# A language-model tower on one core: one rotary rotation for a head's query and key, projected three heads ahead, and softmax reciprocals kept in PSUM

## What is computed

```python
def _rope(x, cos, sin):
    xr, xi = jnp.split(x, 2, -1)
    return jnp.concatenate([xr * c - xi * s, xr * s + xi * c], -1)

def _attn(q, k, v, mask=None):
    s = jnp.einsum('bhqd,bhkd->bhqk', q, k) / np.float32(np.sqrt(HD))
    ...
    return jnp.einsum('bhqk,bhkd->bhqd', jax.nn.softmax(s, -1), v)

qr = _rope((cq @ Wq_rope)..., cos, sin)         # 16 heads, rotary part 64 wide
q = jnp.concatenate([qn, qr], -1)
# three attentions with their own keys; the window's and the selected keys are rotated too;
# their outputs are summed with the weights gate (softmax over three), then projected with Wproj
```

## Time and profile before

| | |
|---|---|
| median of 3 executions | 1830.76 us (1827.94 to 1831.23) |
| the profiled execution | 1832.47 us |
| its span, first to last instruction | 1830.7 us |
| busy share of the span | PE 78%, DVE 78%, ACT 67%, POOL 78% |
| mean granted TensorE clock | 0.959 of full speed |

### The profile page before, as it was taken

How to read it: one execution, slowest core, us unless ns; L and a number is a source line. 1 busy time by engine, 2 the same in 40 slices (tenths; PEclk the granted TensorE clock), 3 DMA queues, 4 the chain that set the end, 5 groups by cost and what they waited for, 6 DMA issues and landing times.

```text
span 1830.7 us, 62295 instructions
## 1 busy us (share of the span) xinstructions
PE 1423.3 (78%) x19368; PEld 1150.3 (63%) x19368; DVE 1436.5 (78%) x4989; ACT 1225.4 (67%) x3280; POOL 1437.0 (78%) x2126
## 2 busy tenths in 40 slices
PE   1041488888888888888888888888888888888778
PEld 0021377767777777777777776777767776766643
DVE  5747678887888788878887888888887888778845
ACT  0041277777777787778877777777767877777644
POOL 6775489877887899789987889788878997899610
PEclk9985699999999999999999999999999999999989
DMA  5110132223222322232222222222222222323200
GB/s 93 22 26 2 35 71 57 52 45 64 52 52 45 71 52 56 46 64 52 53 51 64 53 52 57 56 53 52 55 60 53 52 56 42 60 62 69 54 4 20
DMA packets 327634, 93.11 MB, mean 51 GB/s; under 512 B 321104, under 2 KB 323024, under 8 KB 327520
## 3 DMA queue, kind: packets, MB, share of 16 engines
q1 hardware_dynamic: 324448, 88.48, 24.9%
q0 software_dynamic: 3072, 3.15, 0.9%
HBM read 6.51 MB, written 1.05 MB: 4 GB/s over the span
## 4 chain that ended last, share of the span: by engine, by line
POOL 60%; issue 17%; DVE 10%; PE 8%; POOLq 2%; DMA 2%; ACT 1%; DVEq 0%; ACTq 0%; SPq 0%
POOL big L425 9%; POOL big L424 9%; POOL kparts L460 7%; POOL big L394 5%; POOL vh L480 4%; POOL qparts L446 4%; POOL kparts L457 4%; POOL kk L428 3%; POOL kk L429 3%; POOL qs L428 3%; POOL qs L429 3%; DVE S L1008 3%; POOL osum L473 2%; POOL qparts L449 1%; PE S L1356 1%
## 5 line engine op out<-in xcount | busy, mean ns | idle before, releaser
L635 ACT ACTIVATE big<-S,negm 128x128 f32<-128x128 f32 (+3 forms) x1536 | 577.4, 450 | 196.8 <-DVE negm L1008 195.7
L647 ACT ACTIVATE big<-PT 128x384 f16<-128x384 f32 (+3 forms) x1024 | 426.6, 455 | 150.7 <-PE PT L1381 112.2
L1018 DVE SCALAR_TENSOR_TENSOR big<-PT,big 128x384 f16<-128x384 f32 (+3 forms) x1024 | 472.1, 500 | 39.1 <-ACT big L647 26.3
L1008 DVE CUSTOM_DVE_ANT_0 S<-S,mask_c,unscale 128x128 f32<-128x128 f32 (+3 forms) x512 | 285.1, 557 | 182.8 <-PE S L1356 176.6
L1356 PE MATMUL S<-k1T,qh 128*128 128x128 f16 (+3 forms) x1536 | 296.8, 302 | 113.9 <-DMA qh<-qparts 98.0
L1356 PE MATMUL S<-kh,qh 128*128 128x128 f16 (+1 forms) x3072 | 323.3, 242 | 0.0
L1403 PEld LDWEIGHTS O<-vh,big 128*128 128x128 f16 x8064 | 272.7, 96 | 41.9 <-issue 14.3
L1403 PE MATMUL O<-vh,big 128*128 128x33 f16 x8064 | 283.3, 178 | 14.7 <-DVE big L1030 8.0
L1356 PEld LDWEIGHTS S<-kh,qh 128*128 128x128 f16 x3072 | 229.9, 99 | 56.0
L1388 PE MATMUL PT<-cst,big 128*128 128x128 f32 x1408 | 248.6, 281 | 16.8 <-DVE big L1018 15.1
L1381 PE MATMUL PT<-cst,big 128*128 128x128 f32 x1280 | 232.6, 281 | 19.1 <-DVE big L1018 17.4
(11 more groups left out here) (298 smaller groups left out, 2399.7 us busy)
## 6 DMA issues: line engine op xcount, KB each, us to landing
lat_b<-lat_all SPq DMA_DIRECT2D x8, 448.0 KB, 3.1
qh<-qparts SPq DMA_TRANSPOSE x128, 3.0
kh<-kparts SPq DMA_TRANSPOSE x128, 3.4
xnT_all<-xnT_b SPq DMA_DIRECT2D x14, 128.0 KB, 2.5
xn_b<-xn_all SPq DMA_DIRECT2D x8, 128.0 KB, 2.9
xnT_b<-xnT_all SPq DMA_DIRECT2D x8, 128.0 KB, 2.4
out_dram<-h_all SPq DMA_DIRECT2D x8, 128.0 KB, 2.0
xn_all<-xn_b SPq DMA_DIRECT2D x7, 128.0 KB, 2.0
```

The costliest lines, as they stand in the source:

```text
L635: last = nc.scalar.activation(pr[par][:, lo:lo + n], S[par][:, lo:lo + n], ACT.Exp, bias=negm[par][:, k:k + 1], scale=-1.0)
L647: last = nc.scalar.activation(pT[par][:, 0, lo:lo + n], PT[:, lo:lo + n], ACT.Copy, scale=PSCALE)
L1008: last = v.tensor_tensor_reduce(out=z, in0=z, in1=m, scale=unscale[:] if k == 0 else kfix[:], scalar=3.0e38, op0=ALU.add, op1=ALU.min, acc ...
L1018: v.scalar_tensor_tensor(pT[par][:, 1, lo:lo + n], PT[:, lo:lo + n], PSCALE, pT[par][:, 0, lo:lo + n], ALU.mult, ALU.subtract).then_inc(s[ ...
```

## The change

Three things, in one kernel.

1. **One rotation for a head's query and key.** `qs[par]` and `kk[par]` become two parts of one tile `qk[par]` of 9 tiles. The cosine table gets 9 tiles instead of 5, the sine table is copied into a 9-tile one by two copies on POOL before the first rotation. `prepare` runs one `rope` over all 9 tiles in the place of two, and then splits the key, then the query. The first two heads of each batch still rotate query and key apart.
2. **Three heads ahead.** K and Q of head `h + 3` stand in units 2 and 3 of the turn of head `h`, in the place of head `h + 2` in units 0 and 1. Their copies on ACT and the copy in `high_values` move along. The third head's projections, `qp2` and `kp2`, join the list `LEAD`; `project_rows` moves from units 2 and 3 to units 0 and 1, `half_residual` to unit 1, and PE's wait for it to the start of unit 2. POOL's order within a head is now `low_values`, `branch_sum`, (`normalise`), `prepare`.
3. **Reciprocals in PSUM.** `rinv` is no SBUF tensor any more but 12 unused columns of the PSUM tile `O`.

```diff
-        qs = [sb(f"qs{i}", [P, NT, QW]) for i in range(2)]
-        kk = [sb(f"kk{i}", [P, 5, P]) for i in range(2)]
+        qk = [sb(f"qk{i}", [P, NT + 5, P]) for i in range(2)]
+        qs, kk = [q[:, 0:NT] for q in qk], [q[:, NT:NT + 5] for q in qk]
...
-        rinv = sb("rinv", [P, NT, 3])
...
+        rinv = O[:, NT * 3 * (VD + 1):NT * 3 * (VD + 2)]
...
-        LEAD = ["cq", "qp0", "sel", "k1", "kp0", "qp1", "kp1"]
-        NX = (NH - 2) * 2 + len(LEAD)
+        LEAD = ["cq", "qp0", "sel", "k1", "kp0", "qp1", "kp1", "qp2", "kp2"]
+        NX = (NH - 3) * 2 + len(LEAD)
...
-            def prepare(b, h, hh, par, rows=None):
-
-                x = xbase(b) + h * 2
-                key(par, b, hh, x + x_index(0, "kp"))
-                query(par, b, hh, x + x_index(0, "qp"))
+            def prepare(par, b, hh, x):
+
+                n = rope_count(b, hh, None)
+                g.wait_ge(s["x_evac"], x + 2)
+                rope(qk[par], rt9, cos9, sin9, n)
+                split_key(par, b, hh, n)
+                split_query(par, b, hh, n)
+
+            def cycle(b, h, par, rows=None, add=True):
+
+                low_values(par, b, h + 1)
+                if add:
+                    branch_sum(par, b, h - 1)
                 if rows is not None:
                     normalise(rows, xn_b[:])
-                low_values(1 - par, b, hh - 1)
+                prepare(par, b, h + 3, xbase(b) + h * 2 + x_index(0, "qp"))
...
-                v.reciprocal(rinv[:].rearrange("p t k -> p (t k)").unsqueeze(2), o3[:, :, VD:VD + 1]).then_inc(s["coef_chain"], 1)
+                v.reciprocal(rinv.unsqueeze(2), o3[:, :, VD:VD + 1]).then_inc(s["coef_chain"], 1)
...
-                    if last < 1 and t == 0:
-                        k_proj(h + 2, xb + x_index(0, "kp"))
-                    if last < 1 and t == 1:
-                        q_proj(h + 2, xb + x_index(0, "qp"))
-                    if back is not None and t >= 2:
-                        project_rows(back, p * 2 + t - 2, xb + 2)
+                    if back is not None and t < 2:
+                        project_rows(back, p * 2 + t, xb)
+                    if back is not None and t == 2:
+                        pe.wait_ge(s["h_done"], back * 2 + p + 1)
+                    if xb is not None and t == 2:
+                        k_proj(h + 3, xb + x_index(0, "kp"))
+                    if xb is not None and t == 3:
+                        q_proj(h + 3, xb + x_index(0, "qp"))
```

More of the change, by code:

```diff
@@ L419, in _ @@
                                 f.unsqueeze(2).to_broadcast([P, TILES, hi - lo]), ALU.mult).then_inc(s["lat_done"], 1)
[L421 to L429, removed]
+            g.tensor_copy(sin9[:, 0:NT], sin5[:, 0:NT]).then_inc(s["sin_ready"], 1)
@@ L663, in turn @@
                     u = p * NT + t
-                    if t == 0 and last < 1:
-                        evac_k(p, xb + x_index(0, "kp"), H + 1)
-                    if t == 1 and last < 1:
-                        evac_q(p, xb + x_index(0, "qp"), H + 1)
-                    if t == 2 and last < 2:
+                    if t == 1 and last < 2:
                         high_values(1 - p, b, h + 1)
+                    if t == 2 and xb is not None:
+                        evac_k(1 - p, xb + x_index(0, "kp"), H + 2)
+                    if t == 3 and xb is not None:
+                        evac_q(1 - p, xb + x_index(0, "qp"), H + 2)
                     if nxt is not None:
@@ L724, in behind @@
                 probs(0, 0, b, U)
+                if first:
+                    lead(LEAD.index("qp2"), nxt, b * NH)
+                lead(LEAD.index("kp2"), nxt, b * NH)
                 if not first:
@@ L729, in behind @@
                 probs(2, 2, b, U + 2)
-            for i in range(len(LEAD)):
+            for i in range(LEAD.index("qp2")):
                 lead(i, 0)
@@ L737, in heads @@
             def heads(b, rows=False):
-                with act.Fori(0, NH // 2 - 1) as hp:
+                with act.Fori(0, NH // 2 - 2) as hp:
                     for p in range(2):
                         turn(b, hp * 2 + p, xbase(b) + hp * 4 + p * 2, p, 0, rows=hp if rows and p == 1 else None)
+                turn(b, NH - 4, xbase(b) + (NH - 4) * 2, 0, 0)
+                turn(b, NH - 3, None, 1, 0, rows=NH // 2 - 2 if rows else None)
             def last_heads(b, nxt):
@@ L1123, in turn @@
                         maxima(u + 3, (t + 3) % NT, U + t + 3)
-                    if back is not None and t == 3:
+                    if back is not None and t == 1:
                         half_residual(back, p)
@@ L1448, in turn @@
                     values(u, t, p, U + t, H)
-                if back is not None:
-                    pe.wait_ge(s["h_done"], back * 2 + p + 1)
             def value(b, j):
@@ L1493, in behind @@
                 scores(0, 0, 0, H * NT)
+                if first:
+                    lead("qp2", b, nxt)
+                lead("kp2", b, nxt)
                 if not first:
@@ L1520, in heads @@
                              rows=hp if rows and p == 1 else None)
+                turn(NH - 4, b * NH + NH - 4, xbase(b) + (NH - 4) * 2, 0, 0)
+                turn(NH - 3, b * NH + NH - 3, None, 1, 0, rows=NH // 2 - 2 if rows else None)
             def hidden(b, chunks=(0, 1, 2, 3), between=None):
@@ L1541, in _ @@
             last.then_inc(s["rank_psum"], 1)
-            for kind in LEAD[2:]:
+            for kind in LEAD[2:LEAD.index("qp2")]:
                 lead(kind, 0, 0)
```

69 lines of the change are left out of this document (42 added, 27 removed).

## The result

The changed kernel takes **1761.9 us** (median; the kernel before has 1830.3 in the same series): ratio 0.9635, 95% interval 0.9619 to 0.9651. That is 68 us less; forecast were 76 less, 1755, with a range of 1733 to 1793. The profiled execution has 1769.7 us, with a span of 1767.9. One of the five executions took 1805.5 us, and like it the profiled ones of the experiments `e3`, `e6` and `e8` lie 33 to 44 us above the median of their kernel; in these three the granted clock is down behind the heads, so only what lies ahead of that stretch is read from them.

What follows compares the result with a forecast made beforehand. POOL was taken to bound the kernel at 11.00 us a head, then the PE-DVE-ACT round at 10.35. Savings of 56, 10 and 10 made 76 us, from 1832.5 to 1756.5, as a median 1755; range 1733 to 1793.

Steps and rivals of the forecast that it cites:

- The bound moves from POOL to the round of PE, DVE and ACT: Main case: heads fall from POOL's 11.00 us to the round's 10.35, with POOL at 10.1; chance 0.50.
- The rotation: On POOL: products save 0.42 us, sums 0.26, a gap 0.20; together 0.88 a head, leaving POOL's head at 10.1.
- The round: PE, ACT and DVE links from the end of M3 once round, K and Q included: sum 10.37, taken as 10.35 us.
- The old order was the looser one: The same walk in the old order skips K and Q: 9.2 us a head with a free C, hidden by POOL.
- POOL as the bound: Rival: POOL still bounds every head at 10.1 us because the round's hand-overs overlap; 1737 us, chance 0.17.
- The reciprocals: With a PSUM input C on DVE stops waiting for POOL and takes 0.22 us, 0.47 less; worth nothing in the old order.
- The rival in which C keeps its wait: C on DVE still waits for POOL, so each head has 10.8 us; 1799 us, chance 0.24 shared with the 9-tile rival.
- A batch: Heads and the late turn save 8.0 us a batch, 56 in seven; the batch's first turns 1.5 net, 10 in seven.
- The last batch: POOL gives back 1.75 us per pair of heads, where `normalise` also runs; six pairs make 10 us.
- 9 tiles without a saving: Rival: POOL's instruction over 9 tiles saves nothing, POOL's head 10.8 us; 1799 us, chance 0.24 shared with C's wait.
- Q waiting for K's copy: Slower rival: on PE, Q waits for ACT's copy of K from tile `X`; at 1.0 us of waiting 1858 us, chance 0.05.
- No change: Rival: the losses from Q's waiting just eat the gain; 1831 us, chance 0.04.

Runs made afterwards that it cites:

- e3: The kernel before with only the one rotation over 9 tiles, still two heads ahead, reciprocals in SBUF: 2000.4 us, ratio 1.0930.
- e6: The changed kernel with key and query rotated apart again, still three heads ahead, reciprocals in PSUM: 1804.9 us, ratio 0.9857.
- e8: The changed kernel with three more, unused reciprocals on DVE between C and the product: 1770.4 us, ratio 0.9669.
- e9: The changed kernel with one more POOL copy of 48 columns in every head (0.23 us): 1763.6 us, ratio 0.9645.
- e7: The changed kernel with K between T1 and V0 of unit 0, Q between S0' and T2 of unit 1, `project_rows` in units 2 and 3: 1730.6 us.
- e4: The changed kernel with K and Q back at the starts of units 0 and 1, still three heads ahead: 1735.2 us, ratio 0.9491.
- e10: e7 with POOL's instructions reordered, `branch_sum` split around the key and query splits, casts ahead of differences: 1721.6 us, ratio 0.9409.
- e12: e10 with ACT's copy of the query moved behind H2 of unit 1: 1713.1 us, ratio 0.9366.
- e2: The kernel before with only the reciprocals moved to PSUM: 1830.8 us, ratio 1.0001.
- e1: The changed kernel with the reciprocals back in an SBUF tensor, all else as changed: 1878.9 us, ratio 1.0261.
- e11: The changed kernel with two unused row maxima on DVE between C and the product, 0.66 us of delay: 1918.8 us, ratio 1.0483.
- e7s: e7 with the reciprocals back in an SBUF tensor: 1797.7 us, ratio 0.9822.

## Why the prediction was right, and where it was off

**The bound moves from POOL to the round of PE, DVE and ACT: right, in the middle of the batches.** The wait for the query's DMA went, POOL waits for ACT's copy, and the filler of `e9` is free there. In the last batch POOL stays the bound. With the undone rotation (`e6`) POOL bounds again.

**The rotation: right, a little small.** The products take 1.40 and 1.41 (forecast 1.38), the sums 0.79 (forecast 0.85), the whole 4.65 (4.71). POOL's head without foreign waits is 10.03 (`e7`), against 10.1, and 10.95 with two rotations: 0.92 gained where 0.88 was forecast.

**The round: right, link by link.** From the rows above: M3 1.35; from L1 to K, with T2 and V1 between, 1.76 (forecast 0.63 + 1.04); K 0.43; S1', T3 and V2 2.12; Q 0.66; S2' to M2' 1.30; M2' and L0' 1.75; R, C and the product 1.04. Sum 10.41, the forecast 10.37. The largest miss is 0.09, in the hand-over from L1 to T2: I had counted from L1's first half, but V1 comes behind T2's second part, which waits for the second half. The next round is 10.55, and over eleven heads the mean is 10.46 against 10.35. That makes 0.11 x 11 x 7 = 8 us of the 13 by which the profiled execution's gain fell short of the forecast 76.

**"The old order was the looser one": right in sign, too small in size.** `e4` and `e7` show it, and they land where the prediction had priced POOL as the bound (1737; measured 1735 and 1731). But the walk of 9.2 was too short. With POOL no longer bounding, the order with K and Q in the gaps takes 9.97 on average (`e10`), and 9.74 at its best here (`e12`).

**The reciprocals: the mechanism right, the size wrong.** C falls to 0.17 (0.22 forecast), and in the old order it is worth nothing (`e2`), as written. In the new order the prediction put it at 0.47 us a head, 44 us in all (1799 against 1755); undone it costs 117. Two things had been left out: with 1.41 us on POOL the wait would have grown to 0.7, and the clock falls behind PE's longer waits. The rival in which C keeps its wait was priced at 1799 and would have been 1879. Both errors lie outside of the forecast case, so they didn't touch the time.

**A batch: 8.1 gained, 9.5 forecast.** Eleven heads that are 0.11 longer than forecast make 1.2 of the 1.4 that are missing. PE's waits for the residual, 0.95 and 1.28 in the earlier trace rows, aren't gone: they stand in front of K, and measure 0.46 and 0.18. In the first turn S0' still waits 0.56 for the key's transfer.

```profile
413.32 0.34 PE L1381 MATMUL S<-k1T,qh 128*128 128x128 f16 x3 [0.56 <-DMA kh<-kparts]
...
415.49 0.50 PE L1337 MATMUL X<-wkw,xh 128*128 128x96 f16 x8 [0.46 <-DVE h_all L1132]
...
426.28 0.50 PE L1337 MATMUL X<-wkw,xh 128*128 128x96 f16 x8 [0.18 <-DVE h_all L1132]
```

**The last batch: right where it was argued.** A pair of heads gains 1.90 (1.75 forecast), six pairs 11, and it is POOL's gain, as argued. From the last of the `attended` rows to POOL's last key split the profiled execution gains 9.4; behind that it loses 2.1, which leaves the 7.3. Its granted clock from 1640 to 1700 us is 0.79; in the execution of `e9`, whose work there is the same but for the filler, it is 0.89, and the span is 4.8 shorter (first the changed kernel, then `e9`):

```profile
1640.00:1700.00 60.00, 46.58 (x507) 37.00 (x503) 39.20 (x140) 32.75 (x83) 24.63 (x43) 0.79 0.13 28
```

```profile
1640.00:1700.00 60.00, 42.86 (x508) 33.44 (x503) 41.96 (x151) 32.41 (x83) 25.58 (x46) 0.89 0.14 28
```

That goes some way to explain why this execution lies 7.8 above the median; what decides the clock in that stretch stays open.

**The rivals.** POOL as the bound: out in the middle of the batches, by `e9`. C with its wait, or 9 tiles without a saving: out, by the rows. Q waiting for K's copy: no wait stands ahead of Q. No change: out.

## What to carry to other kernels

Walk the next bound link by link before the first is removed: here it lay 0.5 us behind, and the new place of K and Q, chosen with the rotation, lay on it; the same change with K and Q in PE's idle stretches is 31 us faster. An edit's worth belongs to an order: the same twelve numbers in PSUM were worth 0, 67 and 117 us in three of them. Before an instruction on an in-order queue is made to wait for something later, look at what stands behind it: with `low_values` behind a waiting rotation (`e3`) PE waited 2.44 us for it in the head shown, more than the 0.88 that the rotation saves.

## What the runs showed of the hardware

- **The clock multiplies a wait.** PE waits of 0.4 and 0.6 to 0.8 us in a head left the granted clock at 1.00 in the middle of the batches (the changed kernel), 1.06 to 1.17 and 0.65 to 0.84 brought it to 0.50 for 2 to 3 us in about every second head (`e1`, `e11`). So 0.66 us more on the round (`e11`) cost 1.07 a head on average over eleven heads, and C's 0.7 (`e1`) cost 1.3. Waits of nearly the same length bring the clock down in one head and not in the next; nothing that I found in the rows tells the two apart, and it stays open.
- **C's wait ends with POOL's instruction**: between 430 and 1300 us all 168 rows of C over 0.3 us (the kernel before, `e1`, `e7s`) end 0.02 to 0.04 us behind a POOL instruction, whether that lasts 1.16 or 1.41; with one input in PSUM C took 170 to 171 ns on average in every run. The Trainium skill ("SBUF — State Buffer", Who interferes with whom) says that a VectorE instruction with two SBUF inputs contends with a GpSimd one that reads SBUF, and that the ports they share are an exclusive lock; the runs agree. Its larger latency for a PSUM source ("VectorE: DVE Perf Modes", The TRN2 errata) isn't seen in this instruction: 171 ns with PSUM, 170 at best in the earlier trace rows without.
- **Small DVE instructions overlap.** Three reciprocals of 12 columns, 0.20 us each by their rows, delayed the next instruction by 0.11 in all: they began before C had ended and were not over when the product began (`e8`).
